# Attention logits made on VectorE from neighbour scores spread through DRAM, in a fused graph-attention and expert kernel

## The reference

```python
def gat_layer(x, adj, W, a_self, a_neigh, b):
    feat = jnp.einsum('nf,hfo->hno', x, W)
    attn_self = jnp.einsum('hno,ho->hn', feat, a_self)
    attn_neigh = jnp.einsum('hno,ho->hn', feat, a_neigh)
    e = attn_self[:, :, None] + attn_neigh[:, None, :]
    e = jax.nn.leaky_relu(e, 0.2)
    e = e + MASK_VAL * (1.0 - adj)[None, :, :]
    alpha = jax.nn.softmax(e, axis=-1)
    out = jnp.einsum('hnm,hmo->hno', alpha, feat) + b[:, None, :]
    return jax.nn.elu(out)            # heads side by side: [256, 256]
x = x + tanh(g_xattn) * gat(gat(ctx_512, layernorm(x)), layernorm(x))
x = x + tanh(g_ffn) * moe(layernorm(x))
```

## Time and profile before

| | us |
|---|---|
| median of 3 runs | 438.49 (437.89 to 438.68) |
| the profiled execution | 438.83 |
| its span, first to last instruction | 437.1 |

### The profile page before, as it was taken

The page is one execution under the profiler, slowest core; times in us unless marked ns, Lnnn a source line. Parts: engine busy times, 40 slices in busy tenths (PEclk is TensorE's granted clock), DMA queues, the critical chain, the costliest instruction groups (busy, mean ns, idle before and its releaser), DMA issues.

```text
span 437.1 us, 8093 instructions
## 1 busy us (share of the span) xinstructions
PE 388.4 (89%) x2824; PEld 328.8 (75%) x2825; DVE 257.3 (59%) x814; ACT 243.2 (56%) x520; POOL 90.4 (21%) x100
## 2 busy tenths in 40 slices
PE   3865788698887999997999999999999999999981
PEld 2443556466665777875887889999999999999981
DVE  3799998979978595596367341433434344333440
ACT  4597999999875485641021125555464554645410
POOL 6656050000000004004303000121212212122121
PEclk9999989989999899998999999999999999999998
DMA  6189999200000001001299510122222222221211
GB/s 175 43 337 341 339 351 425 99 0 2 1 1 1 1 1 51 25 0 52 50 424 428 195 26 1 38 39 36 42 47 36 37 36 40 48 38 24 26 19 19
DMA packets 22867, 42.58 MB, mean 97 GB/s; under 512 B 1968, under 2 KB 20976, under 8 KB 21680
## 3 DMA queue, kind: packets, MB, share of 16 engines
q1 hardware_dynamic: 17504, 35.76, 23.8%
q0 software_dynamic: 4080, 5.18, 7.7%
q10 hardware_dynamic: 1248, 1.18, 0.8%
HBM read 24.81 MB, written 17.31 MB: 96 GB/s over the span
## 4 chain that ended last, share of the span: by engine, by line
PE 59%; DVE 22%; ACT 11%; POOL 3%; issue 2%; DMA 1%; ACTq 0%; DVEq 0%; POOLq 0%
PE ps_z L756 13%; PE ps_o L772 11%; PE ps_gu L756 9%; DVE weights L1041 5%; PE ps_pt L608 5%; PE ps_z L601 5%; ACT weights L835 4%; PE ps_gu L601 4%; DVE weights L1036 4%; ACT weights L841 2%; PE ps_gu L608 2%; ACT weights L826 2%; PE ps_pt L520 2%; DVE hidden L1094 2%; DVE gate_silu L1091 2%
## 5 line engine op out<-in xcount | busy, mean ns | idle before, releaser
L442 POOL DMA_INDIRECT out<-y_sb,tile_in x23 | 35.9, 1559 | 157.5 <-DVE y_sb L1280 157.5
L756 PEld LDWEIGHTS ps_z<-tile_t,weights 128*128 128x128 f32 x552 | 65.2, 192 | 1.1
L756 PE MATMUL ps_z<-tile_t,weights 128*128 128x128 f32 x552 | 65.4, 275 | 0.0
L835 ACT ACTIVATE weights<-weights 128x256 f32<-128x256 f32 x128 | 63.4, 509 | 0.1
L932 ACT ACTIVATE weights<-weights 128x2560 f32 x23 | 53.8, 2337 | 6.4 <-issue 6.4
L1091 DVE SCALAR_TENSOR_TENSOR gate_silu<-gate_tanh,ps_z 128x256 f32<-128x256 f32 x66 | 24.5, 372 | 52.3 <-ACT gate_tanh L927 39.0
L772 PE MATMUL ps_o<-weights,hidden 128*128 x230 | 53.7, 381 | 1.6 <-DVE hidden L1094 1.6
L520 PE MATMUL ps_pt<-ident,weights 128*128 128x128 f32 x256 | 35.9, 286 | 13.6 <-ACT weights L841 13.4
L772 PEld LDWEIGHTS ps_o<-weights,hidden 128*128 128x128 f32 x230 | 42.0, 190 | 6.7 <-issue 2.0
L520 PEld LDWEIGHTS ps_pt<-ident,weights 128*128 128x128 f32 x256 | 30.3, 148 | 19.7 <-issue 18.7
L756 PE MATMUL ps_gu<-tile_t,weights 128*128 128x128 f32 x368 | 44.9, 275 | 0.0
(11 more groups left out here) (191 smaller groups left out, 592.5 us busy)
## 6 DMA issues: line engine op xcount, KB each, us to landing
weights<-w_routed SPq DMA_DIRECT2D x8, 1920.0 KB, 17.0
slots<-pad_row SPq DMA_DIRECT2D x9, 1188.0 KB, 13.5
weights<-w_shared SPq DMA_DIRECT2D x1, 3840.0 KB, 13.8
tile_in<-slots SPq DMA_DIRECT2D x23, 132.0 KB, 2.1
out<-y_sb ACTq DMA_DIRECT2D x4, 256.0 KB, 2.2
weights<-x SPq DMA_DIRECT2D x2, 256.0 KB, 4.5
x_in<-x SPq DMA_DIRECT2D x2, 256.0 KB, 5.5
out<-y_sb,tile_in POOLq DMA_INDIRECT x23, 3.8
```

What stands on the lines that cost most here:

```text
L442: pool.indirect_dma_start(out=out, out_offset=bass.IndirectOffsetOnAxis(ap=tile_in[:, slot, ID_COL:ID_COL + 1].bitcast(U32), axis=0), in_= ...
L756: mm = pe.matmul(ps_chunk[c][:, part * cw + i * P:part * cw + (i + 1) * P], ring[r % RING][:, a:a + P], tile_t[:, r % 2, k, :], start=(k = ...
L835: ins = act.activation(v, v, ACT.Exp, bias=neg_max[:, w % AHEAD, i:i + 1], scale=-1.0, accum_out=sums[:, L % PAIR, s:s + 1])
```

## The change

1. Logits without TensorE. Per head the neighbour scores t and 0.2 t are made for each of the 256 nodes (16 rows), and 0.8 s for the own scores s (8 columns). The bent logit max(s + t, 0.2 (s + t)) is ((t + 0.8 s) max 0.2 t) + 0.2 s, and a term that is constant along the row drops out of the softmax. `mask_max` makes it with four VectorE instructions of 256 from `t_wide` (t and 0.2 t on all 128 partitions) and a column of `s_cols`.
2. Spreading. `nodes(L)` (TensorE, into a bank of its own, `ps_n`) and `copy_nodes(L)` (ScalarE, two small copies) give 16 rows of 256; SyncE writes them to a DRAM tensor `t_rows` (16 KB) and reads them back onto all partitions, two transfers of 1 MB, each with its semaphore. There are two buffers; the read for layer L waits until `mask_max` is done with layer L - 2. Layer 0 does not go through DRAM: TensorE spreads t with a broadcast stationary operand (`first_wide`), ScalarE copies it, VectorE scales it.
3. Gone: `scores`, `copy_scores`, `split_scores`, the `pick` patterns.
4. The two banks of `ps_z` are free: graph 0's shared pieces take turns in two banks, and a `gate_up` waits for the piece before the last.
5. Pads. Only the ninth region of `slots` is filled at the start. The pads behind the last row of each of the 8 experts are scattered by GpSimd (8 indirect transfers of 128 rows) when the counts are known, after the last `send_rows`; the tile fetches wait for them.
6. `LATE = 7`: one expert is loaded early and seven late. SyncE's queue has the spreads of layers 1 and 2 before `w_shared`, that of layer 3 before the fill, and those of 4 to 7 behind expert 0.

```diff
+def nodes_at(L):
+    ready = UNITS * (L - 2)
+    if ORDER[L][1] == 1:
+        ready = max(ready, UNITS * (layer_of(ORDER[L][0], 0) + 1) + 2)
+    return ready
+NODES_AT = {nodes_at(L): L for L in range(PAIR, STREAM)}
...
-    return (PIECES * (n - 1) + i) % 3 if n > 0 else 0
+    return (PIECES * (n - 1) + i) % 3 if n > 0 else i % 2
...
-        LATE = 5
+        LATE = 7
...
+            def spread_rows(L):
+                c = L % PAIR
+                sp.wait_ge(t_copied, L)
+                sp.dma_start(t_rows[L], t_few[c][0:T_ROWS, :]).then_inc(st_t, 16)
+                if L >= PAIR:
+                    sp.wait_ge(max_ready, UNITS * (L - 1))
+                sp.wait_ge(st_t, 16 * L)
+                for quad in range(QUADS):
+                    half = KINDS * QUAD
+                    src = t_rows[L, quad * half:(quad + 1) * half, :].rearrange("(o r) n -> o (r n)", o=1)
+                    sp.dma_start(t_wide[c][:, quad * KINDS:(quad + 1) * KINDS, :].rearrange("p k n -> p (k n)"),
+                                 src.to_broadcast([P, half * N])).then_inc(ld_t[c][quad], 16)
...
+            pool.wait_ge(fill_step, 3)
+            pool.wait_ge(pads_ready, 1)
+            for e in range(E):
+                pool.indirect_dma_start(out=slots, out_offset=bass.IndirectOffsetOnAxis(ap=pad_pos[:, e:e + 1], axis=0),
+                                        in_=pad_row, in_offset=None).then_inc(st_pads, 16)
...
-                    if piece > 0:
-                        pe.wait_ge(hid_ready, PIECES * n + piece)
-                    gate_up(n, piece, ps_gu)
+                    if piece >= 2:
+                        pe.wait_ge(hid_ready, PIECES * n + piece - 1)
+                    gate_up(n, piece, ps_chunk[piece_bank(n, piece)])
...
-                if u != 0 and w + UNITS < ALL_UNITS:
-                    scores(w + UNITS)
                 if w > 0:
                     weigh(w - 1)
+                if w in NODES_AT:
+                    nodes(NODES_AT[w])
...
+            def copy_nodes(L):
+                act.wait_ge(nodes_ready, L + 1)
+                if L >= PAIR:
+                    act.wait_ge(max_ready, UNITS * (L - 1))
+                act.activation(s_cols[L % PAIR]..., ps_n[:, N:N + HV * HEADS], ACT.Copy).then_inc(s_copied, 1)
...
             def mask_max(w):
+                if w >= AHEAD:
+                    dve.wait_ge(probs_turned, w - AHEAD + 1)
+                if u == 0:
+                    dve.wait_ge(s_copied, L + 1)
...
+                    dve.wait_ge(ld_t[c][quad], 16 * ((L + 1) // PAIR if c else L // PAIR))
+                for i in range(QUAD):
+                    h = quad * QUAD + i
+                    ins = dve.scalar_tensor_tensor(out=logits[:, w % AHEAD, i * N:(i + 1) * N],
+                                                   in0=t_wide[c][:, KINDS * quad, i * N:(i + 1) * N],
+                                                   scalar=s_cols[c][:, half, h:h + 1],
+                                                   in1=t_wide[c][:, KINDS * quad + 1, i * N:(i + 1) * N], op0=ALU.add, op1=ALU.max)
...
-                dve.wait_ge(z_copied, w + 1)
-                z = logits[:, w % AHEAD, :]
-                dve.scalar_tensor_tensor(out=z, in0=z, scalar=LEAK, in1=z, op0=ALU.mult, op1=ALU.max).then_inc(bent_ready, 1)
```

217 lines of the change are left out of this document (110 added, 107 removed).

## The result

| | before | after |
|---|---|---|
| median, us | 438.49 (436.61 to 438.68, 7 runs) | 434.08 (432.56 to 434.98, 7 runs) |
| the profiled execution, its span | 438.83, 437.1 | 433.88, 431.8 |

The ratio is 0.9915, 95% interval 0.9893 to 0.9938. The change saves 4.4 us. I had forecast 13.8, under a third of which came; the time lies 0.1 us over the upper end of the range, 417 to 434.

What follows compares the result with a forecast made beforehand. ScalarE and VectorE were both near full from 30 to 116 us, TensorE bound 116 to 186. Terms -6 - 7 - 0.8 = -13.8 us on 438.83 gave 425.0, as a median 424.7; range 417 to 434.

Steps and rivals of the forecast that it cites:

- start: Up to the first units' masking: masking begins earlier and a split goes, against a second scaling and dearer bends; -0.8 us.
- first stage: 30 to 116 us, units 4 to 24, no shared pieces: VectorE's sum decides; -6 us, between -8.4 and -2.6.
- second stage: 116 to 186 us, shared pieces: TensorE loses six sets of scores (5.8 us) and some idle time; -7 us.
- the rest: After 186 us: seven late expert loads (32.6 us) and pads stay hidden beside other work; 0 us.
- The bends: VectorE, first stage: four bends of 256 at 0.35 us spacing cost 0.26 us more a unit, +5.2 us for 20.
- the sign: What would show it: a bend spacing near 0.43 instead of 0.35 us would halve the first stage's gain.
- The 5.7 us of waits: First stage: VectorE's bends no longer wait for ScalarE's copy of scores, -5.7 us.
- the poor end that I gave: Second stage: only -3 us instead of -7, if VectorE's order holds TensorE back.
- The spreading: Rows written to DRAM and read back in 7.5 us, hidden by 2.5 us under 10; costed 0, at most +5.
- The late case: Rival: spread rows late for second layers, 2 to 5 us each for layers 3 and 7; 429 to 433, chance 0.08.
- the likeliest case: Whole kernel: all terms come as summed, 424.7 us, own range 418 to 432, chance 0.64.
- The 441: Rival: TensorE, idle without scores, runs at 1.2 GHz through the first stage, 96 us for 86; 441 us, chance 0.08.

Runs made afterwards that it cites:

- the constant: The changed kernel with the column of own scores replaced by the constant 0.5 in the four bends of a unit: 428.54 us, ratio 0.9797.
- the wide bend: The changed kernel with one bend of 1024 per unit instead of four of 256, own scores left out: 424.0 us, ratio 0.9692.

## Why the prediction was wrong in size

Two steps failed, one in each attention stage. By spans:

| term | forecast, us | measured, us |
|---|---|---|
| start | -0.8 | +0.4 |
| first stage | -6 | -2.9 |
| second stage | -7 | -3.0 |
| the rest | 0 | +0.3 |
| sum | -13.8 | -5.3, in medians -4.4 |

- **The bends (the first step that failed).** I took a spacing of 0.35 us, +0.26 a unit, from maskings whose operands are tiles or constants. It was 0.40: +0.47 a unit, 20 x 0.47 = 9.4 us in the first stage for 5.2. I had 0.43 as the upper bound and named it as the sign, but took the low end. By the constant, the spacing for a split was right (0.34) and the column operand is the whole miss of this term. The Trainium skill ("VectorE: DVE Perf Modes", the section on the TRN2 errata, on the read-write bubble) says that many small tiles pay a fixed cost each; an estimate from its table is 58 cycles at 0.96 GHz, 60 ns. The split with a constant agrees in kind, with 0.23 / 3 = 77 ns, and the column is not in it.
- **The first stage: -2.9 for -6.** Between the marks VectorE's busy time rose by 1.7 us (79.1 to 80.8), about -7.9 for the splits and +9.4 for the bends, and its idle time fell by 4.6 (7.2 to 2.6). The removed splits did what I said. The 5.7 us of waits that I took off here were the whole program's: 2.6 of them lay in this stage, and 2.2 more were waits for `score_nodes`, which went with the splits. That error hardly changed the sum.
- **The start: +0.4 for -0.8.** The first bend ran at 12.16, but for 1.67 us, and masking began at 13.98 for 14.34 before. 0.4 of the 1.2 us came.
- **The second stage: -3.0 for -7, the poor end that I gave (the second step that failed).** I had 5.8 us for the scores and 1.2 for idle time. The scores gave theirs: at a clock of 1.00 TensorE needs 59 us here. But I priced the slow clock for the first stage alone and put it at nothing here; it cost 3.3 us in after, 1.7 to 5.0 in five profiles. Of the idle time nothing went: the second bank took away the waits of `gate_up` (4.1 us before), and the first `down`, which I had not looked at, waited 3.72 us for VectorE's order.
- **ScalarE** has 71.7 us of work in the first window where I had 66.5; it does not bind.
- **The spreading.** The write took 1.4 to 1.8 us where nothing stood before it, for 2.2; the first read of a layer 4.4 to 4.8, for the 2.2 + 2.5 of the forecast. That sum was right. The second read, issued 0.4 us later, landed after 6.5 to 8.4. The late case is not the one I named: layer 4's write at 64.03 landed after 11.9 us behind the pads' fill and expert 0, and VectorE waited 0.8 us. With the wide bend it waited 4.0.
- **The last part** was as long, by 0.3 us. Seven loads took 42 us, not 32.6. Before's five took 29.9, 6.0 each, so I could have read 42; the 423 GB/s behind my 4.65 us includes what else runs beside the loads. The first routed tile was turned at 260.96, 8.5 us after the last landing. Two more late loads in before cost 0.7 us, not told from none.
- **The clock.** Slower as feared, 0.85 for 0.96 in the first window, and there without effect as long as VectorE binds, as the likeliest case had it. "Under 2 us" for a few stretches more was too little for the second stage. The 441 did not come.

## What to carry to other kernels

When work moves onto the engine that is next to full, price its instructions in the form they will have, operand kinds included: here 0.06 us by 128, 5 to 6 us in the run with the constant, was over half of the missing gain, and rows of the old kernel had it. Where an engine is busy 94% of a stage, write the stage as its work plus its waits: work that is taken out counts, but a slower clock can take part of it back, and when one wait is covered look for the next on the same engine. A slow clock costs nothing behind a full engine; it costs in the stage that its own engine fills, and comes due elsewhere when the full engine is relieved. And before one profile's mark is read as an effect, see how far it moves between profiles of the same code, here 3.5 us.
